# Attention weights scaled and limited head by head, and their bits turned before the exponent is taken

## The reference, cut to what matters

```python
def log_int_softmax(x, sf, bits=4):
    x_int = x / sf
    x_int = x_int - x_int.max(axis=-1, keepdims=True)
    exp_int, _ = _int_exp(x_int, sf)
    exp_sum = exp_int.sum(axis=-1, keepdims=True)
    ratio = jnp.where(exp_int > 0.0, exp_sum / jnp.maximum(exp_int, 1.0), 2.0 ** 31)
    softmax_out = jnp.round(ratio)
    rounds = round_ln(jnp.maximum(softmax_out, 1.0))
    mask = rounds >= 2.0 ** bits
    qlog = jnp.clip(rounds, 0.0, 2.0 ** bits - 1.0)
    return jnp.where(mask, 0.0, 2.0 ** (-qlog))
...
attn = log_int_softmax(attn, a_scale)
out = jnp.einsum('bhnm,bhmd->bhnd', attn, v)
```

## Time and profile before

| | us |
|---|---|
| median of 3 runs | 1160.63 (1156.34 to 1164.04) |
| the profiled execution's own time | 1158.21 |
| its span, first to last instruction | 1156.4 |
| busy in the span: VectorE | 970.8 (84%) |
| ScalarE | 752.8 (65%) |
| TensorE | 745.9 (65%) |
| GpSimd | 152.6 (13%) |

### The profile page before, as it was taken

One profiled execution on the slowest core, in us unless ns is written; L12 is line 12 of the kernel. 1 busy time (PEld: TensorE's weight loads), 2 busy tenths in 40 slices (PEclk: granted clock), 3 DMA queues, 4 the chain that ended last, 5 costly groups with the idle time before them and its releaser, 6 DMA issues. The chain is left out here.

```text
span 1156.4 us, 23186 instructions
## 1 busy us (share of the span) xinstructions
PE 745.9 (65%) x6175; PEld 527.2 (46%) x6176; DVE 970.8 (84%) x2490; ACT 752.8 (65%) x1304; POOL 152.6 (13%) x265
## 2 busy tenths in 40 slices
PE   4761156574888566666666666666652398699997
PEld 3640044342555333333333433333321286699986
DVE  5777889788888799999999999999999881467666
ACT  0351000594888889999999999999983175355553
POOL 5840000004665000000000000000000630000000
PEclk9985567897999777788788788778755677799999
DMA  5001000000111111000000000110003000455542
GB/s 161 3 2 68 0 0 0 1 0 18 36 37 37 35 27 22 21 21 21 21 21 21 21 21 21 24 22 20 18 6 143 12 1 1 171 188 178 197 169 101
DMA packets 84367, 54.57 MB, mean 47 GB/s; under 512 B 53832, under 2 KB 83304, under 8 KB 84072
## 3 DMA queue, kind: packets, MB, share of 16 engines
q1 hardware_dynamic: 83304, 53.97, 15.3%
q0 software_dynamic: 1024, 0.13, 0.2%
HBM read 11.77 MB, written 3.76 MB: 13 GB/s over the span
## 5 line engine op out<-in xcount | busy, mean ns | idle before, releaser
L1240 DVE SCALAR_TENSOR_TENSOR expo<-expo,con,pow 128x153 f32<-128x153 f32 x480 | 146.1, 375 | 0.7 <-ACT expo L1174 0.7
L1069 PE MATMUL at_pT<-identb,vi 128*128 128x128 bf16 x480 | 62.3, 297 | 88.7 <-ACT vi L1148 88.0
L613 ACT ACTIVATE qi<-pq,biasp,ap 128x306 int16<-128x306 f32 x96 | 47.9, 722 | 94.0 <-PE pq L571 94.0
L1053 PE MATMUL at_rem<-below,identb 128*128 128x459 bf16 x160 | 68.1, 426 | 61.8 <-ACT expo L1174 60.8
L1174 ACT ACTIVATE expo<-at_rem,con 128x459 f32<-128x459 f32 x160 | 96.7, 641 | 15.7 <-PE at_rem L1054 7.9
L882 DVE TENSOR_REDUCE rs_ends<-rs_banks 128x770 f32 (+1 forms) x96 | 91.5, 959 | 14.0 <-PE rs_banks L853 11.9
L802 ACT ACTIVATE rs_banks<-rs_banks 128x770 f32<-128x770 f32 x96 | 76.3, 798 | 25.0 <-PE rs_banks L845 24.4
L1137 ACT ACTIVATE octave<-at_banks,con 128x459 int16<-128x459 f32 x160 | 90.2, 650 | 1.2 <-PE at_banks L708 0.2
L703 PE MATMUL at_banks<-pick,row_top 128*128 128x459 bf16 x160 | 78.1, 488 | 19.6 <-ACT octave L1137 18.0
L1069 PEld LDWEIGHTS at_pT<-identb,vi 128*128 128x128 bf16 x480 | 43.6, 132 | 103.3 <-issue 76.4
L1289 DVE CUSTOM_DVE_ANT_0 weight_top<-weight_top,line 128x2448 uint16<-128x2448 uint16 x64 | 83.8, 1350 | 8.1 <-ACT line L1165 5.8
(11 more groups left out here) (380 smaller groups left out, 2171.5 us busy)
## 6 DMA issues: line engine op xcount, KB each, us to landing
qk<-vt SPq DMA_DIRECT2D x64, 384.0 KB, 3.1
rs_kb<-qk SPq DMA_DIRECT2D x128, 28.7 KB, 1.9
kb<-qk SPq DMA_DIRECT2D x128, 28.7 KB, 2.0
patches<-in_patches SPq DMA_DIRECT2D x4, 768.0 KB, 10.1
vi<-vt SPq DMA_DIRECT2D x32, 96.0 KB, 2.0
out<-vi SPq DMA_DIRECT2D x32, 96.0 KB, 1.7
pj_w<-in_w SPq DMA_DIRECT2D x1, 2304.0 KB, 8.4
qb<-qk SPq DMA_DIRECT2D x128, 6.0 KB, 1.8
```

What stands on the lines that cost most here:

```text
L1053: pe.matmul(out, identb[:, :], bank(below, b), start=True, stop=False)
L1069: mm = pe.transpose(pT[:, slot, j * P:(j + 1) * P], src, identb[:, :])
L1240: ins = v.scalar_tensor_tensor(ex[:, t, :], ex[:, t, :], c(7), pw[:, t, :].bitcast(BF16), ALU.add, ALU.mult, accum_out=tot[:, t:t + 1])
```

## The change

The multiplication by 1.5 and the upper limit move into the scaling. The reciprocal is taken of two thirds of the sum, and a second column per row, `limit`, is 1 or 0.7, by whether the row's sum lies under a bound. `top` is then written row by row: 15 instructions with two column scalars each, multiply by `inv`, take the smaller of `limit`. The two broadcast multiplications and the pass L1278 go. `lines` reads `top` and has a third as its factor.

TensorE turns the high halves of the sums themselves, read from `top` at every second 16-bit place (`high`); the floor of the exponent is taken when the turned group is moved out of PSUM (`exponents`). ScalarE's four index passes go; `corner` copies the image columns of the 12 heads (12x32) and takes the exponent of those of the three both-image rows (3x32). The turned tiles now lie side by side in one tile, `pall`, and VectorE multiplies all of it by 128 in one pass (2316 columns of int16), after the third eviction, in the place of L1281 and L1284. In VectorE's order the transpose and this pass come before the scalings.

```diff
@@ attention, tiles
+        pall = sb("pT_all", [P, H * N + HT * (P + 32)], BF16)
+        ptT = pall[:, 0:H * N].rearrange("p (h n) -> p h n", n=N)
+        piT = pall[:, H * N:H * N + HT * P].rearrange("p (t n) -> p t n", n=P)
+        pjT = pall[:, H * N + HT * P:H * N + HT * (P + 32)].rearrange("p (t n) -> p t n", n=32)
+        high = top[:, :, :].bitcast(BF16).rearrange("p w (n two) -> p w n two", two=2)[:, :, :, 1]
@@ TensorE, turn
-                        pe.wait_ge(pt_done, n * 2 + min(g, 1) + 1)
-                        pe.wait_ge(pi_done, n * 2 + min(g, 1) + 1)
+                        pe.wait_ge(i_done, n * 2 + min(g, 1) + 1)
+                        if g == GROUPS - 1:
+                            pe.wait_ge(pi_done, n + 1)
...
-                            src = pt[:, t, :] if t < RT else ...
+                            src = high[:, t, 0:NT] if t < RT else ...
@@ ScalarE
-                power = lambda out, x: act.activation(out.bitcast(I16), x.bitcast(I16), ACT.Relu, scale=128.0, bias=index[:, 1:2])
+                exponent = lambda out, x: act.activation(out.bitcast(I16), x.bitcast(I16), ACT.Relu, scale=1.0 / 128.0, bias=index[:, 0:1])
-                def indices(n):
...
-                    for h, half in enumerate(halves):
-                        bits = top[:, half, :].bitcast(I16).rearrange("p w (n two) -> p w n two", two=2)[:, :, :, 1]
-                        act.wait_ge(i_done, n * 2 + h + 1)
-                        act.activation(pi[:, half, :].bitcast(I16), bits[:, :, IW:N], ACT.Identity, scale=1.0 / 128.0, bias=index[:, 0:1]).then_inc(pi_done, 1)
-                        act.activation(pt[:, half, :].bitcast(I16), bits[:, :, 0:NT], ACT.Identity, scale=1.0 / 128.0, bias=index[:, 0:1]).then_inc(pt_done, 1)
+                def corner(n):
...
+                    act.wait_ge(i_done, n * 2 + 2)
+                    act.activation(pi[:, :, :].bitcast(I16), high[:, 0:H, IW:N].bitcast(I16), ACT.Copy).then_inc(pi_done, 1)
+                    exponent(pk[:, :, :], high[:, H:RT, IW:N]).then_inc(pj_index, 1)
...
                 def lines(n):
                     for h, half in enumerate(halves):
                         act.wait_ge(w_done, n * 2 + h + 1)
-                        act.activation(flat(line, half), flat(ex, half), ACT.Identity, scale=0.5, bias=index[:, 2:3]).then_inc(y_done, 1)
+                        act.activation(flat(line, half), flat(top, half), ACT.Identity, scale=1.0 / 3.0, bias=index[:, 1:2]).then_inc(y_done, 1)
@@ VectorE, body
-                        v.tensor_scalar(tot[:, :], tot[:, :], 2.0 ** -64, None, ALU.max).then_inc(tot_done, 1)
+                        v.tensor_scalar(inv[:, :], tot[:, :], 2.0 ** -64, 2.0 / 3.0, ALU.max, ALU.mult).then_inc(tot_done, 1)
+                        v.tensor_scalar(limit[:, :], tot[:, :], c(8), LIMIT, ALU.is_lt, ALU.max).then_inc(limit_done, 1)
...
+                    if yj is not None:
+                        nj = yj[0]
+                        v.wait_ge(pj_index, nj + 1)
+                        if not first(nj, 1):
+                            v.wait_ge(pv_done, nj)
+                        v.transpose(pjT.rearrange("p t n -> p (t n)"), pk[:, :, :].rearrange("p t n -> p (t n)")).then_inc(pk_done, 1)
+                        v.wait_ge(ev_done, nj * GROUPS + GROUPS)
+                        v.wait_ge(pk_done, nj + 1)
+                        v.tensor_scalar(pall[:, :].bitcast(I16), pall[:, :].bitcast(I16), 128.0, None, ALU.mult).then_inc(pj_done, 1)
                     if yb is not None:
                         v.wait_ge(inv_done, nb + 1)
-                        for half in halves:
-                            share = inv[:, half].unsqueeze(2).to_broadcast([P, half.stop - half.start, N])
-                            v.tensor_tensor(ex[:, half, :], ex[:, half, :], share, ALU.mult).then_inc(w_done, 1)
...
-                        v.tensor_scalar(top[:, :, :], ex[:, :, :], 1.5, TOP, ALU.mult, ALU.min).then_inc(a_done, 1)
...
+                        v.wait_ge(limit_done, nb + 1)
+                        for t in range(RT):
+                            ins = v.tensor_scalar(top[:, t, :], ex[:, t, :], inv[:, t:t + 1], limit[:, t:t + 1], ALU.mult, ALU.min)
+                            if t + 1 in (HALF, RT):
+                                ins.then_inc(w_done, 1)
```

More of the change, by code:

```diff
@@ L42 @@
 PARTS = 3
-INDEX = 16384
-DEEPEST = 64
-TOP = float(np.float32(2.0 / 3.0 - 2.0 ** -23))
+LIMIT = 0.7
 def ds(start, size):
@@ L933, in attention @@
         ex, top = sb("expo", [P, RT, N]), sb("weight_top", [P, RT, N])
-        tot, inv = sb("total", [P, RT]), sb("inv_total", [P, RT])
-        step, index = sb("octave_step", [P, P], BF16), sb("p_index", [P, 3])
+        tot, inv, limit = sb("total", [P, RT]), sb("inv_total", [P, RT]), sb("weight_limit", [P, RT])
+        step, index = sb("octave_step", [P, P], BF16), sb("p_index", [P, 2])
         topT, row_top = sb("top_rows", [P, B // 2, P], BF16), sb("row_top", [P, 2, P], BF16)
         old = m["vi"].rearrange("p g c -> p (g c)")
-        pt = old[:, 0:RT * P].rearrange("p (t n) -> p t n", n=P)
-        vs = old[:, RT * P:RT * P + 6 * P].rearrange("p (u c) -> p u c", u=2)
-        piT = old[:, RT * P + 6 * P:RT * P + 9 * P].rearrange("p (t n) -> p t n", n=P)
+        vs = old[:, 0:6 * P].rearrange("p (u c) -> p u c", u=2)
         vbs, zero = sb("v_image_row", [P, 2, HT * 4 * HD], BF16), sb("zero_column", [P, 2], BF16)
-        pi, ptT = sb("p_image", [P, RT, 32], BF16), sb("pT_text", [P, H, N], BF16)
-        pjT, pkT = sb("pT_both", [P, HT, 32], BF16), sb("pT_index", [P, HT, 32], BF16)
+        pi, pk = sb("p_image", [P, H, 32], BF16), sb("p_both", [P, HT, 32], BF16)
+        pall = sb("pT_all", [P, H * N + HT * (P + 32)], BF16)
[3 more added lines that the diff above has]
+        high = top[:, :, :].bitcast(BF16).rearrange("p w (n two) -> p w n two", two=2)[:, :, :, 1]
         banks, rem = k.ps("at_banks", [P, 3, 512], F32, st), k.ps("at_rem", [P, 2, 512], F32, st)
@@ L1156, in powers @@
                         if g < 2:
-                            power(ptT[:, 6 * g:6 * g + 6, 0:NT], slot[:, 0:6 * P].rearrange("p (h n) -> p h n", n=P)).then_inc(ev_done, 1)
+                            exponent(ptT[:, 6 * g:6 * g + 6, 0:NT], slot[:, 0:6 * P].rearrange("p (h n) -> p h n", n=P)).then_inc(ev_done, 1)
                         else:
-                            power(ptT[:, :, NT:N], slot[:, 0:3 * P].rearrange("p (h n) -> p h n", n=32)[:, :, ID:32])
-                            power(piT[:, :, :], slot[:, 3 * P:6 * P].rearrange("p (t n) -> p t n", n=P)).then_inc(ev_done, 1)
+                            exponent(ptT[:, :, NT:N], slot[:, 0:3 * P].rearrange("p (h n) -> p h n", n=32)[:, :, ID:32])
+                            exponent(piT[:, :, :], slot[:, 3 * P:6 * P].rearrange("p (t n) -> p t n", n=P)).then_inc(ev_done, 1)
                 def lines(n):
@@ L1189, in body @@
                     if last is not None:
-                        indices(last[0])
-                        powers(last[0], last[1])
+                        corner(last[0])
+                        exponents(last[0], last[1])
                     if mid is not None:
@@ L1203, in _ @@
             def _(v):
-                v.memset(index[:, 0:1], INDEX + DEEPEST - 253.0 - 0.5 + 1.0 / 256.0).then_inc(set_up, 1)
-                v.memset(index[:, 1:2], -128.0 * (INDEX + DEEPEST - 16)).then_inc(set_up, 1)
-                v.memset(index[:, 2:3], 0.5).then_inc(set_up, 1)
+                v.memset(index[:, 0:1], 16.0 - 253.0 - 0.5 + 1.0 / 256.0).then_inc(set_up, 1)
+                v.memset(index[:, 1:2], 0.5).then_inc(set_up, 1)
                 link, inv_step = chained(k, v), m["qa"][:, 1:2]
@@ L1256, in body @@
                         v.wait_ge(tot_done, nb + 1)
-                        v.reciprocal(inv[:, :], tot[:, :]).then_inc(inv_done, 1)
+                        v.reciprocal(inv[:, :], inv[:, :]).then_inc(inv_done, 1)
                     if yf is not None:
@@ L1261, in body @@
                     if yb is not None:
                         v.wait_ge(inv_done, nb + 1)
-                        for half in halves:
-                            share = inv[:, half].unsqueeze(2).to_broadcast([P, half.stop - half.start, N])
-                            v.tensor_tensor(ex[:, half, :], ex[:, half, :], share, ALU.mult).then_inc(w_done, 1)
-                    if yj is not None:
-                        nj = yj[0]
-                        v.wait_ge(pi_done, nj * 2 + 2)
-                        if not first(nj, 1):
-                            v.wait_ge(pj_done, nj)
-                            v.wait_ge(pv_done, nj)
-                        v.transpose(pkT[:, :, :].rearrange("p t n -> p (t n)"), pi[:, H:RT, :].rearrange("p t n -> p (t n)")).then_inc(pk_done, 1)
@@ L1285, in body @@
[L1285 to L1286 removed]
+                        v.wait_ge(limit_done, nb + 1)
[3 more added lines that the diff above has]
```

(2 more changed lines are left out.)

38 lines of the change are left out of this document (12 added, 26 removed).

## The result

The changed kernel takes 1222.8 us (median of 4 runs, 1219.8 to 1224.6) against 1161.2 for the kernel before: a ratio of 1.053 (95% interval 1.049 to 1.058). It is slower, as forecast, but by 5.3% where 2.8% was forecast, and 1222.8 lies above the range of 1169 to 1215.

The account below looks back on a forecast made before the run. VectorE and ScalarE were both taken as full, at 14.19 us a step. +1.08 a step over 30 steps (32.4), +0.8, -0.5 and set-up 0.15 made +33: 1191 profiled, 1193 us as median, 2.8% slower; range 1169 to 1215.

Parts of the forecast that it names:

- 3.06 us: ScalarE's standstill per step ahead of lines: eviction tail 0.11, two handovers of 0.03, x128 pass 0.64, eight scalings 2.25.
- The price of a scaling: VectorE, one head's scaling of 153 float32: 0.27 us from start to start, 0.36 for the last; bounds 0.08 and 0.35.
- B: Scalings on VectorE: 153 odd elements lose the two-per-cycle rate, 0.35 us each; step 15.91, about 1213 us; chance 0.10.
- C: Scalings on VectorE at 0.14 us each: standstill 2.02, step 14.23, time left alone at 1162 us; chance 0.09.
- D: Scalings on VectorE lose their fixed part, 0.08 us each: step 13.75, faster by 13 us, 1148; chance 0.05.
- VectorE's own sum of 14.53: VectorE's work per attention step after the change: 13.82 us before plus 0.71.
- Rival A: ScalarE's wait closes no loop, so VectorE alone sets the attention step: 14.53 us, 1171 us in all; chance 0.10.
- ScalarE's loop becomes 12.21 + 3.06 = 15.27: Attention step: ScalarE's own 12.21 us plus 3.06 of standstill ahead of lines sets the step, above VectorE's 14.53.
- whether seven scalings (1.9) hide the first half of lines from VectorE: VectorE's adds need the first half of lines 1.3 us after the eighth scaling; seven scalings of 1.9 us hide that.
- That wait is in the 14.19 and I keep it: ScalarE's squares wait for TensorE 11.7 us in 28 steps; taken over unchanged within the old step of 14.19 us.
- the powers' wait for the turns: ScalarE's powers wait for TensorE's turns 0.2 us a step; could grow to three times as much, costed at nothing more.
- gave the last steps back 0.5 us: Last two steps, without distances and squares: the shorter way from adds to exponents takes back about 0.5 us.

Follow-up runs that it names:

- e1_pass_after: The changed kernel with VectorE's order exchanged: the 15 scalings come first, the transpose and x128 pass behind them; 1179.6 us, ratio 1.019 to the kernel before.
- e7_after_filler: e1_pass_after with 22 filler matmuls a step on TensorE, results not used; 1181.0 us, ratio 1.017 to the kernel before.
- e4_filler: The changed kernel with 26 filler matmuls of 459 columns in TensorE's idle stretch of each step, results not used; 1201.9 us, ratio 1.037 to the kernel before.

## Why the prediction was wrong in size, point by point

**Right.** The direction and the mechanism: ScalarE stands still ahead of lines for the x128 pass and eight scalings. 3.06 us had been computed with the tail of the last eviction, 2.95 without; 2.98 was measured. The price of a scaling: 15 in 4.12 us, so 0.27 apart and 0.35 for a single one, as read from the earlier trace rows; rivals B, C and D, which hung on another price, did not come in, and neither did the 0.14 of the formula of the Trainium skill ("VectorE: DVE Perf Modes"). The limit column 0.14, the x128 pass 0.68 with its handover, corner 0.69 for 0.79. VectorE's own sum of 14.53: e1_pass_after, where hardly anything holds VectorE up, has 14.57 of work in a step of 14.71. The wait at the x128 pass, 0.56 for some 0.6. Rival A (VectorE alone sets the step) does not describe the changed kernel; it describes e1_pass_after and e7_after_filler. ScalarE's busy time fell by a seventh, as forecast (13.55 to 11.66 us a step), but that was given as its busy share, which fell from 95% to 72%, by a quarter.

**The step that failed** is "ScalarE's loop becomes 12.21 + 3.06 = 15.27". The mean step was 16.18. Its missing 0.9 us:

- *The second half of lines, 0.57.* The prediction asked whether seven scalings (1.9) hide the first half of lines from VectorE, and they do. It did not ask the opposite: the second half of lines waits for the same seven scalings, and the first half, 1.32 long, covers only that much of their 1.89. The number was in the earlier trace rows, the rule in the diff (`w_done` twice).
- *The squares, 0.49* (0.91 for 0.42). The prediction took the squares' wait for TensorE over unchanged ("That wait is in the 14.19 and I keep it"). It hangs on TensorE's clock, and the change lengthened TensorE's idle stretch ahead of these remainders from 1.1 to 2.4 us to 6.2. "TensorE is idle a third of the step" stood as the reason to add nothing for TensorE; this idleness is what goes with the lower clock. e4_filler shows it: 0.85 us a step come back, 0.68 at the squares and 0.19 at the distances.
- *Distances, 0.15:* 2.83 us instead of 2.68 in the mean; in half of the steps they take 3.0 instead of 2.63 (620.06 to 623.06), also at the lower clock.
- *Against it, 0.3:* corner is 0.1 shorter, and the powers' wait for the turns (0.2 a step in the earlier trace rows) is gone, where a growth had been held possible.

12.21 + 3.06 + 0.57 + 0.49 + 0.15 - 0.3 = 16.18. The terms are read from the time lines and agree with the mean step to 0.1 or so each. Thirty steps of 0.9 more are 27 of the 30 us by which the forecast missed.

**The ends.** The prediction gave the last steps back 0.5 us. Instead the way from the last distances to the end grew by 6.1, of which 5.2 lie ahead of the projection's long maximum: the last two steps hold the same waits, and VectorE comes late to the projection. Moving 4.0 us of its work into the hole took 4 us off that span. The first three steps took 2.8 us longer (442.41 - 402.38 against 437.77 - 400.51) for 1.9 predicted, 0.8 for the second and 1.08 for the third.

**How the 62 us divide.** With the order mended 19 to 21 remain (e1_pass_after), so 41 to 43 are the order. Of what remains, VectorE's path is 0.5 us a step, 15 us; the rest is in the ends. The clock has no share of its own to be added: it costs 0.85 us a step where ScalarE's path sets the step (e4_filler) and nothing where VectorE does (e7_after_filler).

Not settled: how the 0.6 us between e4_filler (15.33) and VectorE's own 14.7 divides between the two halves of lines; no run changed the size of the halves alone, so the 0.57 of the second half is read from the time line (the same in all 28 steps) and from the sum, not from an experiment of its own. Open too is why the layer norm took 5 to 6 us more in three of the profiled executions.

## What to carry to other kernels

When a change moves a pass between engines that run in fixed orders, write down for each wait what is queued in front of the instruction that releases it, in both directions and for each part of a split; here one pass put ahead of the scalings instead of behind them cost some 42 of 62 us. A wait within a stage is a property of the engine waited for: if the change makes that engine idle longer, price its work again at the lower clock. And time saved on an engine is worth something only once it is handed work of the bound: the freed 2 us of ScalarE were worth nothing in the variants that gave it no new work, and 1.1% when it took over five rows of the scaling.

## What the runs showed of the hardware that was not expected

- TensorE at the lower clock after an idle stretch of 6.1 to 6.2 us in 28 of 28 steps (459 columns in 0.57 to 0.59 us). Before, after 1.1 to 2.4 us, it was at the higher one in 24 of 28 (0.37) and at the lower one in four, behind waits of 2.2 to 2.3. Filler matmuls in the long stretch held the mean granted clock at 1.00 in 28 steps.
- Turning 128x128 tiles of 16-bit values taken at every second place cost as much as turning dense ones: six in 0.51 us at the higher clock in both kernels, 0.055 apart.
- Scalings of 153 float32 columns with two column scalars on VectorE are 0.27 us apart (15 in 4.12 us).
